# A four-layer graph network on one core: x and the first adjacency matrix are loaded ahead of the later layers' weights, whose preparation moves into the aggregations of three later steps

## The chip, the cores and the metric

The kernel runs on one core of a Trainium2 chip. The metric is the time of one execution on the device in microseconds (us); lower is better. Engines are named as in the profile: PE is TensorE's matmuls and PEld its loads of the stationary operand, DVE is VectorE, ACT ScalarE, POOL GpSimd, SP SyncE (which here only issues DMAs). The prediction below was written from the profile of the kernel before, with the changed kernel not yet built.

## The reference

```python
# x (8, 1024, 128), adj (8, 1024, 1024) of zeros and ones, mask (8, 1024), 4 layers
h = x
for i in range(4):
    hw = einsum('bnc,cd->bnd', h, weight[i])
    m = einsum('bjn,bjd->bnd', adj, hw)
    gx = m @ w_ih[i].T + b_ih[i]
    gh = h @ w_hh[i].T + b_hh[i]
    xr, xz, xn = split(gx, 3)
    hr, hz, hn = split(gh, 3)
    r, z = sigmoid(xr + hr), sigmoid(xz + hz)
    n = tanh(xn + r * hn)
    h = (1 - z) * n + z * h
out = layernorm(x + h * mask[:, :, None])
```

## The kernel before

The kernel forms m @ w_ih.T as (adj.T h) (weight w_ih.T). So a layer needs one joined matrix wx = weight[l] w_ih[l].T and one transposed matrix wh = w_hh[l].T, both 128 x 384, and both are held as a sum of a high part (rounded to the fast fp32r type) and a low part (the rest). The states are split in the same way. An adjacency block is exact in the high part alone; VectorE checks this by OR-ing the bits of every block into `low` (`check_adj`, L720), and a general path at the end runs only if a low bit was set.

Graphs are worked in four pairs, and a pair in 8 steps (`STEPS = 2 * L`): step g works on layer g // 2 of graph g % 2. A step is:

- `aggregate`: S = adj.T h in two banks `p_S`, one for each half of the 1024 nodes, from 8 adjacency blocks of 128 rows. There are 32 products of 512 columns (h high and h low). In steps 0 and 1 of the first pair the blocks are the outer loop (L380, L382), since they are still arriving; elsewhere the halves are (L398).
- ScalarE copies S to `S_hi`, and VectorE forms `S_lo` (`s_low`).
- `transpose_former` (L369): the new state of the step before is transposed back into `p_tr`, for its next aggregation; ScalarE and VectorE split it into `nat_hi` and `nat_lo`.
- `gates`, for each half: 9 products with the state (banks `p_r`, `p_z`, `p_hn`) and 9 with S (L408 to L410). ScalarE takes the sigmoids and the tanh, VectorE forms t (L851, L857), GpSimd forms (h - n) and z (h - n) (L1003, L1007), VectorE adds the new state (`new_state`, L796), and ScalarE and VectorE split it (`h_high`, `h_low`).

Every engine runs its own list of instructions in order, written out by hand, and waits on counted semaphores: `wait_ge(name, n)` holds the engine until n events have been counted. What stands between the main operations are fillers: `fill` on VectorE issues one check of an adjacency block (one after S_lo of half 0, one in the middle of the gates, one at the end of the step), and `take_adj` on ScalarE casts a block from `adj_in` to `adj_hi`. `adj_in` has one buffer for each of the 8 blocks, so block j of the next graph is loaded by SP only when block j of the last one was both cast and checked.

The start, ahead of step 0, in the order of the lists: SP issues the weights of the four layers (`load_layer`, three DMAs each), the rows of biases and the mask, x of graph 0, the 8 adjacency blocks of graph 0, x of graph 1, and then the blocks of graph 1 one by one. TensorE transposes 7 blocks of 128 x 128 for each layer (`transpose_weights`) and multiplies the transposed weight with w_ih (`join_weights`, 384 columns, in full fp32). VectorE copies the transposed matrices to SBUF (`copy_weights`, L689), ScalarE writes the high parts (`split_w_hh`, `split_joined`) and VectorE the low ones. `transpose_x` transposes x (L349), and its parts go to `hT_hi` and `hT_lo` (`take_xT`; `xT_done` counts them). The start uses gate banks and state buffers that are free until then (`p_start`, `places_start`).

In steps 0 and 1 of the first pair ScalarE casts all blocks of graph 0 and the even blocks of graph 1; VectorE casts the odd blocks of graph 1 (`take_adj1`, L731).

Of the kernel before, what the change touches and what calls it, by code (L numbers as in the profile page):

```python
# [32 lines left out]
def gnn_kernel(nc, x, adj, nodemask, weight, w_ih, w_hh, b_ih, b_hh, out):  # L33
# [13 lines left out]
    with ctx:  # L47
# [49 lines left out]
        p_start = [(p_r, p_z), (p_S[0], p_S[1]), (p_hn, p_xn), (p_r, p_z)]  # L97
        p_rows = p_start[L - 1][1][:, G * C:]

        def flat(t):  # L100
# [4 lines left out]
        places_start = [work[:, 0:2].rearrange("p a b c -> p (a b c)")[:, 0:N], hT[:, 1],  # L105
                        y[:, 0].rearrange("p a b -> p (a b)"), y[:, 1].rearrange("p a b -> p (a b)")]
        w_nat = [t[:, 0:(1 + 2 * G) * C].rearrange("p (q d) -> p q d", d=C) for t in places_start]

        w_tr = work[:, 2:4].rearrange("p a b c -> p (a b c)")[:, 0:L * (1 + G) * C].rearrange("p (l d) -> p l d", l=L)
        bias_rows, mask_rows = (t[:, N - P:N] for t in places_start[0:2])  # L110
# [8 lines left out]
        start_joined = sem("start_joined")  # L119
        start_hi = sem("start_hi")  # L120
        start_lo = sem("start_lo")
        rows_out = sem("rows_out")
# [3 lines left out]
        adj1_ready = sem("adj1_ready")  # L126
# [92 lines left out]
        def wait_adj(eng, graph, j, graph1=False):  # L219

            if graph1:
                if j % 2:
                    eng.wait_ge(adj1_ready, j // 2 + 1)
                else:
                    eng.wait_ge(adj_ready, NB + j + 2)
            else:
                eng.wait_ge(adj_ready, NB * graph + j + 1)
# [5 lines left out]
        def _(sp):  # L233
# [5 lines left out]
            for l in range(L):  # L239
                load_layer(l)  # L240
# [24 lines left out]
            def body(p, first, last):  # L265
                if first:

                    sp.wait_ge(start_tr, L)
# [43 lines left out]
        def _(pe):  # L312
            pe.wait_ge(ident_made, 1)

            def transpose_weights(l):
                px, ph = p_start[l]
                pe.wait_ge(w_in[l], 48)
                if l == L - 1:

                    pe.wait_ge(start_lo, 1)  # L320
# [3 lines left out]
                if l == L - 1:  # L324
                    pe.wait_ge(rows_in, 48)
# [86 lines left out]
            def gates(p, g, h, first):  # L412
# [10 lines left out]
                if prior:  # L423
                    pe.wait_ge(r_act, HS * p + k)
# [622 lines left out]
```

## Time and profile before

| | us |
|---|---|
| three runs | 572.51, 572.16, 570.96 |
| median | 572.16 |
| profiled execution, its own time from its first to its last instruction (the span) | 570.9 |
| TensorE busy in it | 544.4 (95%) |
| VectorE busy | 431.5 (76%) |
| ScalarE busy | 302.0 (53%) |
| GpSimd busy | 227.1 (40%) |

The span runs from the first to the last instruction of the only core; no time around it is listed for the profiled execution. It lies at the lower end of the three runs. In a timeline a row gives the start and the duration of an instruction in us; "idle before <-releaser" in brackets is how long its engine stood idle ahead of it and who ended that. Instructions of one engine overlap a little, since the next is begun while the last results of the former are written.

### The profile page before, as it was taken

What the parts mean: (1) busy time and instruction counts of PE and PEld (TensorE: products, weight loads), DVE (VectorE), ACT (ScalarE), POOL (GpSimd) and SP (SyncE); (2) the same over time, 40 slices, a digit from 0 to 9 for tenths busy, and PEclk for the clock granted to TensorE, in tenths of its full rate; (3) what the DMA queues carried; (4) which work ended last, traced back from release to release, by engine and by line L of the source; (5) the groups of instructions that cost most, each with busy time, mean ns of one, the idle gap of its engine ahead of it and who ended that gap; (6) DMA issues with size and microseconds to landing.
All of it is one profiled execution on the core that took longest, in us unless ns stands there. A gap on an engine that the chain in (4) does not pass through costs nothing.

```text
span 570.9 us, 7455 instructions
## 1 busy us (share of the span) xinstructions
PE 544.4 (95%) x2536; PEld 446.3 (78%) x2536; DVE 431.5 (76%) x726; ACT 302.0 (53%) x454; POOL 227.1 (40%) x156
## 2 busy tenths in 40 slices
PE   5899999999999999999999999999999999999970
PEld 4567888888888888888888888888888888888860
DVE  3998787875778888877667889887577898675475
ACT  3864444447775434545876454445877444444432
POOL 0054334443265444433266443333364633433302
PEclk9999999999999999999999999999999999999995
DMA  7972233002500109401600017701520013000002
GB/s 233 394 240 75 74 111 110 1 0 105 191 1 1 39 22 331 127 0 53 243 0 0 0 37 232 245 0 37 174 84 0 2 37 111 0 1 0 1 1 76
DMA packets 38125, 48.39 MB, mean 85 GB/s; under 512 B 1656, under 2 KB 29904, under 8 KB 38096
## 3 DMA queue, kind: packets, MB, share of 16 engines
q1 hardware_dynamic: 38096, 48.02, 25.3%
q8 instruction: 16, 0.26, 0.2%
q14 instruction: 13, 0.11, 0.1%
HBM read 43.82 MB, written 4.19 MB: 84 GB/s over the span
## 4 chain that ended last, share of the span: by engine, by line
PE 89%; DVE 7%; ACT 1%; issue 1%; DMA 1%; SPq 0%; POOL 0%; DVEq 0%; ACTq 0%
PE p_S L398 38%; PE p_r L408 5%; PE p_r L410 5%; PE p_r L409 5%; PE p_z L408 5%; PE p_z L410 5%; PE p_z L409 5%; PE p_tr L369 5%; PE p_hn L408 2%; PE p_hn L410 2%; PE p_hn L409 2%; PE p_xn L408 2%; PE p_xn L410 2%; PE p_xn L409 2%; DVE low L720 2%; PE p_tr L349 1%
## 5 line engine op out<-in xcount | busy, mean ns | idle before, releaser
L1003 POOL TENSOR_TENSOR work<-hT,work 128x512 f32<-128x512 f32 x62 | 99.1, 1598 | 284.1 <-ACT work L565 283.9
L398 PE MATMUL p_S<-adj_hi,nat_hi 128*128 128x512 f32 x480 | 187.4, 390 | 0.0
L398 PE MATMUL p_S<-adj_hi,nat_lo 128*128 128x512 f32 x480 | 186.9, 389 | 0.0
L398 PEld LDWEIGHTS p_S<-adj_hi,nat_hi 128*128 128x128 f32 x480 | 90.1, 188 | 18.6
L398 PEld LDWEIGHTS p_S<-adj_hi,nat_lo 128*128 128x128 f32 x480 | 90.1, 188 | 18.5
L720 DVE TENSOR_TENSOR low<-low,adj_in 128x1024 int32<-128x1024 int32 x64 | 94.3, 1473 | 0.5
L1007 POOL TENSOR_TENSOR work<-work 128x512 f32<-128x512 f32 x62 | 88.4, 1426 | 4.9
L851 DVE SCALAR_TENSOR_TENSOR work<-p_hn,bias,work 128x512 f32<-128x512 f32 x64 | 47.9, 749 | 55.0 <-ACT work L565 55.0
L565 ACT ACTIVATE work<-p_r,bsum 128x512 f32<-128x512 f32 x64 | 44.1, 689 | 73.5 <-PE p_r L410 73.4
L796 DVE TENSOR_TENSOR hT<-work 128x512 f32<-128x512 f32 x64 | 43.9, 686 | 30.4 <-POOL work L1007 30.0
L565 ACT ACTIVATE work<-p_z,bsum 128x512 f32<-128x512 f32 x64 | 44.1, 689 | 41.0 <-PE p_z L410 41.0
L523 ACT ACTIVATE hT_hi<-hT 128x512 fp32r<-128x512 f32 x48 | 30.3, 632 | 65.6 <-DVE hT L796 65.6
L680 DVE TENSOR_TENSOR hT_lo<-hT,hT_hi 128x512 fp32r<-128x512 f32 x48 | 46.8, 975 | 18.8 <-ACT hT_hi L523 16.8
L523 ACT ACTIVATE S_hi<-p_S 128x512 fp32r<-128x512 f32 x64 | 38.0, 593 | 43.2 <-PE p_S L398 38.1
L523 ACT ACTIVATE adj_hi<-adj_in 128x1024 fp32r<-128x1024 f32 x60 | 60.3, 1050 | 0.0
L565 ACT ACTIVATE work<-work,bias 128x512 f32<-128x512 f32 x64 | 46.3, 724 | 22.2 <-DVE work L857 22.2
L680 DVE TENSOR_TENSOR S_lo<-p_S,S_hi 128x512 fp32r<-128x512 f32 x64 | 43.6, 682 | 8.3 <-ACT S_hi L523 8.3
L857 DVE TENSOR_TENSOR work<-p_xn,work 128x512 f32<-128x512 f32 x64 | 43.8, 685 | 5.3
L369 PE MATMUL p_tr<-ident,hT 128*128 128x128 f32 x256 | 38.6, 273 | 3.4 <-DVE hT L796 3.4
L369 PEld LDWEIGHTS p_tr<-ident,hT 128*128 128x128 f32 x256 | 31.7, 140 | 11.7 <-issue 3.6
L995 POOL TENSOR_TENSOR hT<-hT_hi,hT_lo 128x512 f32<-128x512 f32 x16 | 25.7, 1627 | 28.1 <-DVE hT_lo L680 28.1
L680 DVE TENSOR_TENSOR nat_lo<-p_tr,nat_hi 128x512 fp32r<-128x512 f32 x48 | 32.8, 683 | 3.7 <-ACT nat_hi L523 3.4
(130 smaller groups left out, 915.5 us busy)
## 6 DMA issues: line engine op xcount, KB each, us to landing
adj_in<-in_adj_dram SPq DMA_DIRECT2D x64, 512.0 KB, 5.4
x_in<-in_x_dram SPq DMA_DIRECT2D x8, 512.0 KB, 11.2
y<-in_x_dram SPq DMA_DIRECT2D x8, 512.0 KB, 5.0
out_dram<-y SPq DMA_DIRECT2D x7, 512.0 KB, 3.3
out_dram<-y SPq DMA_DIRECT2D x2, 256.0 KB, 3.0
y<-in_L_gnn_w_ih_dram SPq DMA_DIRECT2D x2, 192.0 KB, 3.4
y<-in_L_gnn_w_hh_dram SPq DMA_DIRECT2D x2, 192.0 KB, 4.1
work<-in_L_gnn_w_ih_dram SPq DMA_DIRECT2D x1, 192.0 KB, 2.6
```

Of the source, the lines that this page charges most:

```text
L369: last = nc.tensor.transpose(p_tr[h][:, i, :], hT[:, g % 2, n0:n0 + P], ident[:, :])
L398: last = nc.tensor.matmul(p_S[h][:, :], part[:, s, j], adj_hi[:, s, j, half(h)], start=(j == 0 and part is nat_hi), stop=(j == NB - 1 and ...
L408: nc.tensor.matmul(bank[:, :], w_h[:, l, cols], v_h, start=start, stop=False)
L409: nc.tensor.matmul(bank[:, :], w_h[:, l, cols], v_l, start=False, stop=False)
L410: return nc.tensor.matmul(bank[:, :], w_l[:, l, cols], v_h, start=False, stop=stop)
L523: return nc.scalar.activation(dst, src, ACT.Copy)
L565: nc.scalar.activation(dst, bank, func, bias=b).then_inc(made, 1)
L680: return nc.vector.tensor_tensor(dst, src, hi.bitcast(F32), ALU.subtract)
L720: nc.vector.tensor_tensor(low[:, :], low[:, :], adj_in[:, j].bitcast(I32), ALU.bitwise_or).then_inc(adj_checked, 1)
L851: nc.vector.scalar_tensor_tensor(t_sb[:, h], p_hn[:, :], bias[:, 1, G * l + 2:G * l + 3], r_sb[:, h], ALU.add, ALU.mult).then_inc(t_mul, 1)
L1003: nc.gpsimd.tensor_tensor(t_sb[:, h], hT[:, s, half(h)], n_sb[:, h], ALU.subtract).then_inc(d_sub, 1)
L1007: nc.gpsimd.tensor_tensor(t_sb[:, h], z_sb[:, h], t_sb[:, h], ALU.mult).then_inc(d_mul, 1)
```

## The change

SP loads layer 0's weights, then the adjacency blocks of graph 0, the rows of biases and mask, x of graph 1, layer 1's weights, the blocks of graph 1, and layers 2 and 3 behind them. x of graph 0 is loaded by a DMA that ScalarE issues. Ahead of step 0 only layer 0 is transposed and joined. Layer 1 is done inside the aggregation of step 1, layers 2 and 3 inside those of steps 2 and 3, in the banks `p_tr` and in work or y buffers. The 9 products of step 0's first half with the state stand between the first blocks of the aggregation. The odd blocks of graph 0 are cast by VectorE (`take_odd`), and checks 4 to 7 of graph 0 stand among the work of step 0. The core of the diff:

```diff
-        p_start = [(p_r, p_z), (p_S[0], p_S[1]), (p_hn, p_xn), (p_r, p_z)]
+        p_start = [(p_xn, p_hn)] + [tuple(p[:, :, :].rearrange("p i c -> p (i c)") for p in p_tr)] * (L - 1)
...
# SP
-            for l in range(L):
-                load_layer(l)
+            load_layer(0)
+            for j in range(NB):
+                sp.dma_start(adj_in[:, j], adj_v[0, j]).then_inc(adj_loaded[j], 16)
...
-            sp.dma_start(x_in[:, 0], x_v[0]).then_inc(x_loaded[0], 16)
-            for j in range(NB):
-                sp.dma_start(adj_in[:, j], adj_v[0, j]).then_inc(adj_loaded[j], 16)
-            sp.dma_start(x_in[:, 1], x_v[1]).then_inc(x_loaded[1], 16)
+            sp.dma_start(x_in[:, 1], x_v[1]).then_inc(x_loaded[1], 16)
+            load_layer(1)
             for j in range(NB):
-                wait_adj(sp, 0, j)
+                wait_adj(sp, 0, j, True)
                 sp.wait_ge(adj_checked, j + 1)
                 sp.dma_start(adj_in[:, j], adj_v[1, j]).then_inc(adj_loaded[j], 16)
+            load_layer(2)
+            sp.wait_ge(start_joined, 2)
+            load_layer(3)
...
-                    sp.wait_ge(start_tr, L)
+                    sp.wait_ge(start_joined, L)
...
# TensorE
             transpose_weights(0)
-            transpose_weights(1)
+            transpose_x(0, 0, True)
             join_weights(0)
-            transpose_weights(2)
-            join_weights(1)
-            transpose_weights(3)
-            join_weights(2)
-            transpose_x(0, 0, True)
-            join_weights(3)
...
+                        if s == 0 and j < G:
+                            state_product(p, 0, 0, j, first)
+                        elif s == 1 and j == 3:
+                            pe.wait_ge(xT_done, 4)
+                            transpose_weights(1)
+                        elif s == 1 and j == 6:
+                            join_weights(1)
...
+                        if first and g in (2, 3) and (h, j) == (0, 1):
+                            transpose_weights(g)
                     last.then_inc(s_done, 1)
+                    if first and g in (2, 3) and h == 0:
+                        join_weights(g)
...
+                    if first and h == 0 and g < L:
+                        pe.wait_ge(start_lo, g + 1)
                     transpose_h(p, g - 1, h)
...
# ScalarE
+            act.dma_start(x_in[:, 0], x_v[0]).then_inc(x_loaded[0], 16)
...
-                        places = ((), (0,), (2, 4), (6,)) if first else ((), (4, 5), (6, 7), ())
+                        places = ((), (), (0,), (2,)) if first else ((), (4, 5), (6, 7), ())
...
+                    if first and g == 1:
+                        take_adj(0, 1, 4, True)
+                        split_w_hh(1)
+                        take_adj(0, 1, 6, True)
+                        split_joined(1)
+                    elif first and g in (2, 3):
+                        split_w_hh(g)
                     s_high(p, g, 0)
+                    if first and g in (2, 3):
+                        split_joined(g)
...
+                        if first and k == 0:
+                            split_x(0, 1, True)
...
# VectorE
+                        if first and g == 1:
+                            take_xT(0, 1)
+                            copy_weights(1)
+                            take_odd(1, 7)
+                        elif first and g in (2, 3):
+                            copy_weights(g)
                         new_state(p, g - 1, 1)
                         if first and g == 1:
-                            take_adj1(7)
+                            split_w_hh(1)
+                            split_joined(1)
...
                     s_low(p, g, 0)
+                    if first and g in (2, 3):
+                        split_w_hh(g)
+                        split_joined(g)
+                    if first and g == 0:
+                        take_rows()
...
                     s_low(p, g, 1)
+                    if first and g == 0:
+                        check_adj(0, 0, 4)
...
                             if first and g == 0:
-                                take_adj1(1)
+                                split_x(0, 1)
+                                take_odd(1, 1)
                     if first and g == 0:
-                        take_adj1(3)
+                        check_adj(0, 0, 5)
+                        take_odd(1, 3)
...
                     if first and g == 0:
-                        take_adj1(5)
+                        check_adj(0, 0, 6)
+                        take_odd(1, 5)
+                        check_adj(0, 0, 7)
...
-            for j in range(NB - 2):
-                check_adj(0, 0, j, True)
-            take_xT(0, 0)
+            copy_weights(0)
+            split_x(0, 0)
+            split_w_hh(0)
+            dve.wait_ge(xT_hi, 1)
+            lo(hT_lo[:, 0, half(0)], flat(p_tr[0]), hT_hi[:, 0, half(0)]).then_inc(xT_done, 1)
+            take_odd(0, 1)
+            split_joined(0)
+            dve.wait_ge(xT_hi, 2)
+            lo(hT_lo[:, 0, half(1)], flat(p_tr[1]), hT_hi[:, 0, half(1)]).then_inc(xT_done, 1)
+            take_odd(0, 3)
+            check_adj(0, 0, 0, True)
+            take_odd(0, 5)
+            check_adj(0, 0, 1)
+            take_odd(0, 7)
+            check_adj(0, 0, 2)
+            check_adj(0, 0, 3)
             pairs(dve, body)
...
```

New or changed helpers that it calls:

```python
def take_rows():                       # VectorE
    dve.wait_ge(rows_tr, 1)
    nc.vector.tensor_copy(bias[:, :, :].rearrange("p a b -> p (a b)"), p_rows[:, 0:2 * L * G])
    nc.vector.tensor_copy(mask[:, :], p_rows[:, 2 * L * G:2 * L * G + B * NB]).then_inc(rows_out, 1)
    dve.wait_ge(rows_out, 1)
    nc.vector.tensor_tensor(bsum[:, :], bias[:, 0], bias[:, 1], ALU.add).then_inc(rows_out, 1)

def split_w_hh(l):                     # VectorE
    dve.wait_ge(start_hh, l + 1)
    lo(wh_lo[:, l], p_start[l][1][:, 0:G * C], wh_hi[:, l])

def split_joined(l):                   # VectorE
    dve.wait_ge(start_hi, l + 1)
    lo(wx_lo[:, l], p_start[l][0][:, 0:G * C], wx_hi[:, l]).then_inc(start_lo, 1)

def take_odd(graph, j):                # VectorE
    dve.wait_ge(adj_loaded[j], 16 * (graph + 1))
    nc.vector.tensor_copy(adj_hi[:, graph, j], adj_in[:, j]).then_inc(adj_odd, 1)
```

## Rows read from the trace of the kernel before

**Rows 1.** The page of the kernel before, part 1: busy time and share by engine.

```profile
PE 544.4 (95%) x2536; PEld 446.3 (78%) x2536; DVE 431.5 (76%) x726; ACT 302.0 (53%) x454; POOL 227.1 (40%) x156
```

**Rows 2.** Windows, 55.5 to 540 us. Stretch, length, busy by engine, PEclk, DMA share, GB/s.

```profile
55.50:72.00 16.50, 16.50 (x79) 13.60 (x78) 13.29 (x16) 7.57 (x13) 6.60 (x5) 1.00 0.29 96
120.00:540.00 420.00, 420.00 (x1969) 347.39 (x1969) 317.49 (x539) 232.43 (x345) 181.78 (x122) 1.00 0.21 70
```

**Rows 3.** Timeline of the start, all engines. Start, duration (us), engine, line, operation, idle.

```profile
4.78 0.88 PE L322 MATMUL p_r<-ident,work 128*128 128x128 f32 x3 [4.78 <-DMA work<-in_L_gnn_w_hh_dram]
...
6.62 0.69 DVE L689 COPY work<-p_r 128x512 f32<-128x512 f32 x1 [4.65 <-PE p_z L331]
...
9.68 0.85 PE L322 MATMUL p_hn<-ident,y 128*128 128x128 f32 x3
...
14.50 0.81 PE L337 MATMUL p_hn<-work 128*128 128x384 f32 x2
...
17.42 4.86 ACT L523 ACTIVATE adj_hi<-adj_in 128x1024 fp32r<-128x1024 f32 x5
...
18.60 7.87 DVE L720 TENSOR_TENSOR low<-low,adj_in 128x1024 int32<-128x1024 int32 x6
```

**Rows 4.** Timeline of TensorE (PE), 25 to 75 us.

```profile
25.99 0.39 PE L382 MATMUL p_S<-adj_hi,nat_lo 128*128 128x512 f32 x1
...
29.37 0.39 PE L408 MATMUL p_r<-S_hi,wx_hi 128*128 128x512 f32 x1
...
43.32 0.50 PE L380 MATMUL p_S<-adj_hi,nat_hi 128*128 128x512 f32 x1 [1.77 <-DVE adj_hi L731]
...
46.18 0.60 PE L369 MATMUL p_tr<-ident,hT 128*128 128x128 f32 x4
...
55.34 0.39 PE L398 MATMUL p_S<-adj_hi,nat_hi 128*128 128x512 f32 x1
...
62.60 0.60 PE L369 MATMUL p_tr<-ident,hT 128*128 128x128 f32 x4
...
71.75 0.39 PE L398 MATMUL p_S<-adj_hi,nat_hi 128*128 128x512 f32 x1
```

**Rows 5.** Timeline of VectorE (DVE), 27 to 92 us.

```profile
34.86 1.79 DVE L731 CAST adj_hi<-adj_in 128x1024 fp32r<-128x1024 f32 x1
...
40.59 1.00 DVE L680 TENSOR_TENSOR hT_lo<-hT,hT_hi 128x512 fp32r<-128x512 f32 x1 [0.70 <-ACT hT_hi L523]
...
59.18 2.31 DVE L720 TENSOR_TENSOR low<-low,adj_in 128x1024 int32<-128x1024 int32 x1
...
61.41 0.68 DVE L796 TENSOR_TENSOR hT<-work 128x512 f32<-128x512 f32 x1
62.02 0.68 DVE L680 TENSOR_TENSOR S_lo<-p_S,S_hi 128x512 fp32r<-128x512 f32 x1
...
63.40 1.22 DVE L720 TENSOR_TENSOR low<-low,adj_in 128x1024 int32<-128x1024 int32 x1
...
66.80 0.75 DVE L851 SCALAR_TENSOR_TENSOR work<-p_hn,bias,work 128x512 f32<-128x512 f32 x1 [0.98 <-ACT work L565]
...
77.76 0.68 DVE L796 TENSOR_TENSOR hT<-work 128x512 f32<-128x512 f32 x1
```

**Rows 6.** Windows of the start, the same columns as Rows 2.

```profile
0.00:4.00 4.00, 0.00 (x0) 0.00 (x0) 0.97 (x2) 1.49 (x2) 0.75 (x7) 1.00 0.42 123
3.00:4.00 1.00, 0.00 (x0) 0.00 (x0) 0.00 (x0) 0.00 (x0) 0.00 (x0) 1.00 0.96 284
16.00:22.00 6.00, 5.45 (x23) 3.44 (x22) 5.79 (x9) 6.00 (x8) 0.00 (x0) 1.00 1.03 419
```

**Rows 7.** Timeline of ScalarE (ACT), the first S_hi.

```profile
26.02 0.60 ACT L523 ACTIVATE S_hi<-p_S 128x512 fp32r<-128x512 f32 x1 [0.88 <-PE p_S L382]
```

**Rows 8.** DMA issues between 48 and 70 us: transfer, count, KB each, us to landing.

```profile
adj_in<-in_adj_dram SPq DMA_DIRECT2D x4, 512.0 KB, 3.2
```

**Rows 9.** Timeline of GpSimd (POOL), the operation ahead of 61.41.

```profile
58.79 1.62 POOL L1007 TENSOR_TENSOR work<-work 128x512 f32<-128x512 f32 x1
```

More of the change, by code:

```diff
@@ L410, in product, with state_product, gates @@
                 return nc.tensor.matmul(bank[:, :], w_l[:, l, cols], v_h, start=False, stop=stop)
-            def gates(p, g, h, first):
+            def state_product(p, g, h, q, first):
                 l, s = divmod(g, 2)
                 k = 2 * g + h
-                if l == 0:
-                    pe.wait_ge(xT_done, 4 * p + k + 1)
-                else:
-                    pe.wait_ge(h_split, HS_IN * p + k - 4 + 1)
-                state = (hT_hi[:, s, half(h)], hT_lo[:, s, half(h)])
+                if q == 0:
+                    if l == 0:
+                        pe.wait_ge(xT_done, 4 * p + k + 1)
+                    else:
+                        pe.wait_ge(h_split, HS_IN * p + k - 4 + 1)
+                    if first and k == 0:
+                        pe.wait_ge(start_lo, 1)
+                if not (first and k == 0):
+                    pe.wait_ge((r_act, z_act, t_mul)[q], HS * p + k)
+                state = (hT_hi[:, s, half(h)], hT_lo[:, s, half(h)])
+                last = product((p_r, p_z, p_hn)[q], (wh_hi, wh_lo), l, q, state, True, q == G - 1)
+                if q == G - 1:
+                    last.then_inc(hn_done, 1)
+            def gates(p, g, h, first, begun=False):
+                l, s = divmod(g, 2)
+                k = 2 * g + h
                 fed = (S_hi[:, h], S_lo[:, h])
                 prior = not (first and k == 0)
-                if prior:
-                    pe.wait_ge(r_act, HS * p + k)
-                product(p_r, (wh_hi, wh_lo), l, 0, state, True, False)
-                if prior:
-                    pe.wait_ge(z_act, HS * p + k)
-                product(p_z, (wh_hi, wh_lo), l, 1, state, True, False)
-                if prior:
-                    pe.wait_ge(t_mul, HS * p + k)
-                product(p_hn, (wh_hi, wh_lo), l, 2, state, True, True).then_inc(hn_done, 1)
+                if not begun:
+                    for q in range(G):
+                        state_product(p, g, h, q, first)
                 pe.wait_ge(s_split, HS * p + k + 1)
@@ L459, in body @@
                     if g == 0 and first:
-                        pe.wait_ge(start_lo, L)
-                        pe.wait_ge(rows_out, 2)
+                        transpose_rows()
                     for h in range(2):
                         transpose_former(p, g, h, first)
-                        gates(p, g, h, first)
+                        gates(p, g, h, first, first and g == 0 and h == 0)
             pairs(pe, body)
@@ L530, in split_w_hh @@
                 act.wait_ge(start_tr, l + 1)
[L531 to L534 removed]
+                copy(wh_hi[:, l], p_start[l][1][:, 0:G * C]).then_inc(start_hh, 1)
             def split_joined(l):
@@ L542, in take_adj @@
                 act.wait_ge(adj_loaded[j], 16 * (2 * p + s + 1))
-                copy(adj_hi[:, s, j], adj_in[:, j]).then_inc(adj_ready, 2 if first and s == 1 else 1)
+                copy(adj_hi[:, s, j], adj_in[:, j]).then_inc(adj_ready, 2 if first else 1)
             def split_x(p, s, first):
@@ L618, in body @@
                             take_former(p, g - 1, 1)
+                        if first and k == 0:
+                            split_x(0, 1, True)
                         gate(n_sb[:, h], t_sb[:, h], t_add, n_act, ACT.Tanh, bias[:, 0, G * l + 2:G * l + 3], p, k)
@@ L812, in body @@
                 checks = [(p, 1, j) for j in range(NB)] + [(p + 1, 0, j) for j in range(NB) if not last]
-                if first:
-                    checks = [(0, 0, NB - 2), (0, 0, NB - 1)] + checks
                 def fill(g):
-                    if checks and (g or (first and checks[0][1] == 0)):
+                    if checks and g:
                         check_adj(*checks.pop(0))
@@ L840, in body @@
                     s_low(p, g, 1)
+                    if first and g == 0:
+                        check_adj(0, 0, 4)
                     for h in range(2):
```

95 lines of the change are left out of this document (37 added, 58 removed).

## The prediction

> **What bounds the kernel now.** I read the page first: TensorE is busy 95% of the span, VectorE 76% [rows 1]. That is a mean, so I cut the span into stretches. From 55.5 us on TensorE has no gap at all: 16.50 of 16.50 us, and 420.00 of 420.00 later [rows 2]. So a microsecond that TensorE loses or wins ahead of the gate products of step 3 (numbered from 0) reaches the end whole, and nothing behind it gives it back. Up to 55.5 us it idles: first it waits for the weights (4.78 us), then the first aggregation ends late, and the second stops 1.77 us for a cast on VectorE [rows 3, 4]. In the timeline of VectorE the reader is to see the checks of adjacency blocks: six in a row take 7.87 us, a lone one takes 1.22, and one that meets a GpSimd operation 2.31 us [rows 3, 5].
>
> **The sum is made on TensorE's marks** [rows 4]: gate products of step 1 begin (with a transposition) at 46.18, step 2's aggregation at 55.34 (9.16 later), its gates at 62.60 (7.26 later), step 3's aggregation at 71.75.
>
> **Part 1, start to the first aggregation.** Layer 0's weights (0.46 MB) now share the DMA engines with x (0.52 MB), issued by ScalarE. Such an issue isn't in the trace. Bounds: the weights land at 4.78 as before, or after all 0.98 MB; some 0.49 MB (123 GB/s over 4 us) had moved by 4.0 us and 0.28 MB go per us then [rows 6], so 5.7. I take 5.6, since both move rows of 128 floats, and 6.5 for x. The Trainium skill ("DMA: Bandwidth & Descriptors", Issuing engines are not separate DMA queues) says that transfers of several issuing engines interleave on the same DMA engines; by it 5.6 is nearer than 4.78, and no row of this trace shows two issuers.
>
> TensorE: 7 weight and 8 x transpositions at the slow rate, 0.21 us each (0.85 for 3 with the latency of the last, 0.42) [rows 3], the join between; done by 9.6. ScalarE: nat_hi 1.0, wh_hi 0.5, two halves of x transposed (waiting for TensorE) to 9.5, then the cast of block 0, 0.97 (4.86 for five), so the aggregation begins near 10.5. It has 32 products and now 9 state products between them: 41 at 0.2275 (7.26 us for 32 [rows 4]) is 9.3 us, and 1.0 more for what still runs at the slow clock: end 20.8. The blocks don't bound it: 5.17 MB in all, the last 4.2 at 0.42 MB per us (419 GB/s) [rows 6], land by about 16.1. VectorE's list ahead of it is copy 0.7, nat_lo 1.15, three splits of weights and two of x (2.7), four casts (2.4), four checks (4.9), with one GpSimd wait, from 7.4 to some 19.7: no bound either. Before, the last of these products started at 25.99 [rows 4]. So far the gain is some 5.6 us, and because the 9 state products are done, the first product on S starts near 21.8 where it started at 29.37: 7.6 us earlier.
>
> **Part 2, to the end of step 1's aggregation: VectorE takes most of it back.** Only 4 of 8 checks are done by then, and the casts and splits come in between. Behind block 3 of step 1 TensorE now waits for xT_done 4 ahead of the transpositions of layer 1's weights. On VectorE that split stands behind everything of step 0. It starts at 21.15 (half 0 ends some 0.3 before half 1, and S_hi takes 0.60 [rows 7]). A 512-wide operation is followed after 0.61 by the next (61.41, 62.02 [rows 5]), so: two S_lo 1.2, the bias rows 0.4 (three small ones), two pairs of t operations 2.9 (0.75 and 0.68, with small gaps [rows 5]), nat_lo 1.2, checks 4 to 7 at 1.15 4.6, casts 1, 3, 5 at 0.6 1.8, state 0.6, its split 0.65, two splits of x transposed 1.2: 14.6 us. Waits: a cast took 1.79 and a check 2.31 where GpSimd runs, 1.1 to 1.2 more than alone [rows 5]; two of the seven such operations give 2.1 us, since GpSimd has four operations in this stretch. For ScalarE it waits 1.0 (nat_hi of x 1 and the state's split, the latter as 0.70 before [rows 5]). Sum 17.7: xT_done 4 at 38.8. Bounds: 35.7 with no wait, 43 if each of the seven pays 1.1.
>
> Behind it TensorE does 7 transpositions (4 took 0.60 with the latency of the last [rows 4]; I take 0.9 with the change of mode), blocks 4 to 7 (3.64) and the join (0.32; a pair had 0.81 with latency [rows 3]): end 43.6. Block 7's load follows check 7 (37.6) by 3.2 [rows 8], its cast ends at 41.7, no bound. The joined product goes through ScalarE (0.5) and VectorE (0.5), on which the next transposition waits (start_lo 2): 43.95 against 46.18 before. **Gain 2.2 us.** The unfilled rest is a new idle stretch of TensorE: block 2's cast on ScalarE stands behind the new state's split and ends near 35.0, while block 1 is done at 30.8.
>
> **Part 3, steps 2 and 3: TensorE pays in the solid stretch.** Each aggregation gets 7 transpositions behind block 1 and the join behind half 0. The join waits for copy_weights(g), which stands on VectorE behind the check that closes the former step. In the trace that check starts at 59.18, is held by GpSimd's operation of 58.79 to 60.41, and what follows starts at 61.41, 6.07 us after the aggregation began at 55.34; in the next step 77.76, 6.01 after 71.75 [rows 4, 5, 9]. These marks hang on TensorE's own last gates, so they move with it. The copy takes 0.69 [rows 3] and the join can start at 6.85; TensorE is there at 3.64 + 0.75 = 4.4. Stall 2.4 us, nothing is left behind it to fill it. Aggregation then: 6.85 + 0.35 + 3.64 = 10.8 against 7.26: **3.6 us for each step, 7.2 for both.** Of this 2.3 is the moved work itself. Bounds: no stall 2.3; nothing in the rows lets it be over 2 x 3.6 while VectorE's order stands. The splits (start_lo) are ready at 9.0, ahead of 10.8, so the gates don't wait.
>
> **What costs nothing.** Layer 2's loads follow check 7 and land before step 2 (3 to 6 us of cover); layer 3's wait for the second join, near 43, and land by 48, 20 us ahead of use. The loads of y and of graph 2 now stand on SP's queue behind the fourth join (about 80 us) instead of the fourth transposition; the first reader of graph 2 is the check that ends step 3, at about 96, and a load takes some 3 to 6 us. The x loads behind them wait for graph 1's last check, as before. If that cover were gone, a VectorE wait of a few us would come in step 3.
>
> **Sum:** -2.2 + 7.2 = +5.0 on the profiled execution's span of 570.9, so 575.9. Its span lies 1.3 below the median of the runs shown, 572.16; the forecast for a median is 577.1.
>
> **Rivals.**
> 1. *The clock falls* (14%). At the start a transposition had 0.42 us of latency and 0.21 of pace, later 4 of them have 0.60 in all [rows 3, 4]: the low and the high level, 1.2 and 2.4 GHz, though the granted clock reads 1.00 in both [rows 2, 6]. The 1.77 us gap at 43.3 didn't bring the low level back [rows 4]. The new gap of about 4 us (30.8 to 35.0) and the one of 2 us after it are longer. If the low level comes back, the 4.9 us of work from 38.8 to 43.6 takes up to twice as long, and with the other gaps I price it at 3 to 5: 581. The Trainium skill ("TensorE: Matmul & The Clock Gate", Why this matters for your kernels) warns that a long idle gap between bursts throttles the clock again. By that rule this rival is the forecast; no row here has a gap so long.
> 2. *The joins are not late* (13%): VectorE reaches each copy within 3.6 us of the aggregation's start, because the closing check meets no GpSimd operation and its predecessor no wait. For: the 1.1 us of lock is removable. Against: that alone gives 5.0, still 0.6 too late. Then +2.3 - 2.2 = +0.1: 572.3, no change.
> 3. *Other side: VectorE doesn't hold step 1* (9%). With xT_done 4 ready by 32 us, the start-up gain of 7.6 would reach step 2 but for the moved layer 1 work. It decides from there: 6.8 us earlier than 38.8 turns +5.0 into -1.8. Then 570 or a little less. Against: 14.6 us of bare work start at 21.15, so this needs both a much earlier aggregation and work that I count twice.
> 4. *More locks* (12%): every check and cast of step 1 meets GpSimd: xT_done 4 up to 43, gain 2.2 turns into a loss of 2: 581.
>
> **Chances.** Forecast, 575 to 580: 52%. Rival 1 14, rival 4 12, rival 2 13, rival 3 9. About 0.3%, 1.7 us, is what a measurement of this kernel tells from no change. Faster: rival 3 and a little of 2, 10%. Same: the rest of 2 and the low edge, 14%. Slower 76%. The range 572.0 to 581.5 leaves out rival 3 and the far ends of 1 and 4.
>
> **What would show it.** Right: first aggregation product near 10.5 us; a TensorE gap of 3 to 4 us before block 2 of step 1 for ScalarE's adj_hi, and another for hT_lo ahead of the weights' transpositions near 38 us; gates of step 1 near 44; then in each of steps 2 and 3 one gap of about 2.4 us ahead of the 384-column join, released by VectorE's copy, and aggregations 10.8 long; no gap later. Wrong: those two gaps missing (the copy came early), TensorE at half rate behind 35 us, or gates of step 1 at 40 or earlier.

## The result and the profile after

| | us |
|---|---|
| kernel before, five runs beside it | 572.16 median (570.86 to 572.85) |
| changed kernel, five runs | 580.25 median (579.88 to 583.26) |
| ratio | 1.0159, 95% interval 1.014 to 1.0178 |
| span of the profiled execution (583.26, the slowest of the five) | 581.4 |

Slower by 8.1 us: inside the range of 572.0 to 581.5, 3.1 above the forecast, and just above the band of 575 to 580 that the forecast's chance was given for. A run's time is its span and 1.8 us around it. So the profiled execution before, with a span of 570.9, was one of about 572.7 us, 0.6 above the median of 572.16, and not at the lower end of the runs, as it had seemed; the forecast is not moved by this, since its sum is a difference. The page of the changed kernel, busy time and the row of the granted clock over 40 slices:

```profile
PE 547.6 (94%) x2536; PEld 449.7 (77%) x2536; DVE 434.1 (75%) x730; ACT 298.4 (51%) x450; POOL 226.8 (39%) x156
...
PEclk9979899999999999999999999999999999999995
```

TensorE is busy 3.2 us longer than in [rows 1] for the same 2536 instructions, so 7.3 of the 10.5 us between the two spans are time in which it stands idle. Slices 3 and 5 of the clock's row (29 to 44 and 58 to 73 us) show where it also ran slowly. Windows of those stretches and of the rest (columns as in [rows 2]):

```profile
36.00:44.00 8.00, 6.86 (x21) 5.30 (x22) 5.52 (x8) 4.22 (x7) 2.50 (x2) 0.57 0.58 177
44.00:60.00 16.00, 15.71 (x77) 12.68 (x76) 11.87 (x17) 8.42 (x15) 4.57 (x3) 1.00 0.12 35
60.00:68.00 8.00, 5.80 (x18) 4.03 (x17) 7.34 (x9) 1.60 (x3) 1.61 (x1) 0.79 0.01 2
...
100.00:540.00 440.00, 440.00 (x2063) 364.35 (x2063) 338.16 (x562) 241.59 (x360) 188.91 (x125) 1.00 0.22 71
```

From 100 us on TensorE is solid, as before. Timeline of TensorE:

```profile
6.59 0.87 PE L324 MATMUL p_xn<-ident,work 128*128 128x128 f32 x3 [6.59 <-DMA work<-in_L_gnn_w_hh_dram]
...
11.74 0.70 PE L375 MATMUL p_S<-adj_hi,nat_hi 128*128 128x512 f32 x1 [0.44 <-ACT adj_hi L538]
...
22.49 0.51 PE L415 MATMUL p_r<-S_hi,wx_hi 128*128 128x512 f32 x1 [0.59 <-DVE S_lo L698]
...
37.06 0.79 PE L375 MATMUL p_S<-adj_hi,nat_hi 128*128 128x512 f32 x1 [5.05 <-ACT adj_hi L538]
...
40.92 0.90 PE L324 MATMUL p_tr<-ident,y 128*128 128x128 f32 x3
...
45.44 0.81 PE L333 MATMUL p_tr<-y 128*128 128x384 f32 x2
...
47.47 0.63 PE L364 MATMUL p_tr<-ident,hT 128*128 128x128 f32 x4 [0.29 <-issue]
...
63.38 1.64 PE L333 MATMUL p_tr<-y 128*128 128x384 f32 x2 [2.20 <-DVE y L707]
...
65.25 0.63 PE L401 MATMUL p_S<-adj_hi,nat_lo 128*128 128x512 f32 x1
65.68 0.63 PE L401 MATMUL p_S<-adj_hi,nat_hi 128*128 128x512 f32 x1
...
69.45 0.60 PE L364 MATMUL p_tr<-ident,hT 128*128 128x128 f32 x4
...
85.33 0.91 PE L333 MATMUL p_tr<-y 128*128 128x384 f32 x2 [2.14 <-DVE y L707]
...
89.76 0.60 PE L364 MATMUL p_tr<-ident,hT 128*128 128x128 f32 x4
```

These are the marks of [rows 4]: the first product on S came at 22.49 (before 29.37), the gates of step 1 at 47.47 (46.18), of step 2 at 69.45 (62.60), of step 3 at 89.76 (79.00). Behind that mark 491.6 us are left, before 491.9: nothing is given back. Three of the four gaps foretold are there: 5.05 us for ScalarE's `adj_hi` in step 1 (3 to 4 had been forecast), and 2.20 and 2.14 ahead of the joins of steps 2 and 3, for VectorE's copy. The fourth, for `hT_lo` near 38 us, is not: behind the first gap blocks 2 and 3 run at half rate and last until the transpositions at 40.92. The products at 65.25 and 65.68 stand 0.43 apart instead of 0.23, and the granted clock of 60 to 68 us is 0.79: TensorE at its low level, 1.2 GHz, behind a gap. VectorE's timeline in steps 0 to 2:

```profile
27.69 1.79 DVE L745 CAST adj_hi<-adj_in 128x1024 fp32r<-128x1024 f32 x1
...
31.98 1.75 DVE L745 CAST adj_hi<-adj_in 128x1024 fp32r<-128x1024 f32 x1
33.66 1.74 DVE L810 TENSOR_TENSOR hT<-work 128x512 f32<-128x512 f32 x1
...
39.58 1.28 DVE L698 TENSOR_TENSOR hT_lo<-p_tr,hT_hi 128x512 fp32r<-128x512 f32 x2
...
60.43 2.30 DVE L734 TENSOR_TENSOR low<-low,adj_in 128x1024 int32<-128x1024 int32 x1
62.65 0.68 DVE L707 COPY y<-p_tr 128x512 f32<-128x512 f32 x1
```

The last two are the stall: the copy of layer 2's weights behind a closing check of 2.30 us. The first three, two casts and the new state, are prolonged from 0.7 us each while GpSimd works. The timeline of GpSimd has the operation that the closing check met, and that of ScalarE the arrival of x, and the cast that ends the long gap:

```profile
60.04 1.61 POOL L1050 TENSOR_TENSOR work<-work 128x512 f32<-128x512 f32 x1
```

```profile
5.29 1.06 ACT L538 ACTIVATE nat_hi<-x_in 128x1024 fp32r<-128x1024 f32 x1 [2.54 <-DMA x_in<-in_x_dram]
...
35.44 0.63 ACT L538 ACTIVATE hT_hi<-hT 128x512 fp32r<-128x512 f32 x1 [3.74 <-DVE hT L810]
35.97 1.04 ACT L538 ACTIVATE adj_hi<-adj_in 128x1024 fp32r<-128x1024 f32 x1
```

A check alone takes 1.22 [rows 5]. The Trainium skill ("SBUF — State Buffer", Who interferes with whom) says that a VectorE operation with two SBUF inputs contends with a GpSimd operation that reads SBUF. The trace agrees: GpSimd ends at 61.65, and the check, which began at 60.43, ends 1.08 later.

### The profile page after: what moved, and what is told of

Its sections match the earlier page's. It is cut to its first block, busy times and chain, and to the rows that moved or that the text cites. A ratio compares the mean times of both kernels' runs of the same rounds, so it can differ in the third digit from the quotient of the medians.

```text
span 581.4 us, 7459 instructions
## 1 busy us (share of the span) xinstructions
PE 547.6 (94%) x2536; PEld 449.7 (77%) x2536; DVE 434.1 (75%) x730; ACT 298.4 (51%) x450; POOL 226.8 (39%) x156
## 4 chain that ended last, share of the span: by engine, by line
PE 88%; DVE 6%; ACT 2%; issue 1%; DMA 1%; POOL 1%; SPq 0%; DVEq 0%; POOLq 0%
PE p_S L401 36%; PE p_r L415 5%; PE p_r L417 5%; PE p_r L416 5%; PE p_z L415 5%; PE p_z L417 5%; PE p_z L416 5%; PE p_tr L364 5%; PE p_hn L415 2%; PE p_hn L417 2%; PE p_hn L416 2%; PE p_xn L416 2%; PE p_xn L415 2%; PE p_xn L417 2%; DVE low L734 1%
## 5 line engine op out<-in xcount | busy, mean ns | idle before, releaser
L401 PE MATMUL p_S<-adj_hi,nat_hi 128*128 128x512 f32 x480 | 189.4, 395 | 0.0
L538 ACT ACTIVATE adj_hi<-adj_in 128x1024 fp32r<-128x1024 f32 x56 | 56.7, 1049 | 2.1 <-DMA adj_in<-in_adj_dram 2.1
```

Source lines behind the costliest of these rows:

```text
L401: last = nc.tensor.matmul(p_S[h][:, :], part[:, s, j], adj_hi[:, s, j, half(h)], start=(j == 0 and part is nat_hi), stop=(j == NB - 1 and ...
L538: return nc.scalar.activation(dst, src, ACT.Copy)
```

## The experiments

All marks in one table: start of the gates of steps 1, 2 and 3 in the profiled execution, its span, and the median of the runs. Behind the gates of step 3 every kernel here has 490.7 to 491.9 us left, so an edit is worth what the third mark shows.

| kernel | step 1 | step 2 | step 3 | span | median |
|---|---|---|---|---|---|
| before | 46.18 | 62.60 | 79.00 | 570.9 | 572.16 |
| changed | 47.47 | 69.45 | 89.76 | 581.4 | 580.25 |
| changed, a second execution profiled | 46.92 | 67.33 | 87.61 | 579.2 | |
| copies early | 46.59 | 64.75 | 82.80 | 574.4 | 575.85 |
| block 2 first | 48.02 | 70.05 | 90.36 | 581.4 | 583.15 |
| step 1 reordered | 46.06 | 68.00 | 88.28 | 579.8 | 580.95 |
| gaps filled | 47.17 | 67.53 | 87.80 | 578.5 | 580.11 |
| copies early, step 1 reordered | 45.81 | 63.97 | 82.03 | 573.5 | 575.45 |
| short checks | 43.43 | 63.81 | 84.08 | 575.5 | 578.29 |
| casts on ScalarE | 43.85 | 61.96 | 80.02 | 571.8 | 573.60 |
| checks ahead of x | 47.06 | 65.17 | 83.26 | 574.9 | 576.50 |
| layer 2 in step 1 | 43.53 | 59.95 | 78.02 | 569.4 | 571.13 |

### Copies ahead of the closing check

```diff
 # VectorE: step g, behind its last gate work
+                    if first and g in (1, 2):
+                        copy_weights(g + 1)
                     fill(g)                      # the closing check
...
-                        elif first and g in (2, 3):
-                            copy_weights(g)
```

> Edit: VectorE's copies of the transposed weights of layers 2 and 3 stand ahead of the check that closes the step before, not behind it. Theory 1 (the joins wait for that order): the two stalls ahead of the 384-column join (2.20 and 2.14 us in the profile after) go, and with the first of them the half-rate stretch behind it (about 1.9 us): 574 to 576 us, from 580.25. Theory 2 (the join would wait anyway, for the copy itself or for GpSimd, and only the moved work costs): less than 1 us. Theory 3 (the gap goes but the clock falls all the same, since it hangs on something else in step 2): 576 us with a half-rate stretch left in step 2.

Median 575.85 (575.12 to 576.23), ratio to before 1.0069 (1.005 to 1.0087): 4.4 us off the changed kernel. VectorE and TensorE in step 2, two timelines:

```profile
59.60 0.68 DVE L707 COPY y<-p_tr 128x512 f32<-128x512 f32 x1
60.20 1.70 DVE L734 TENSOR_TENSOR low<-low,adj_in 128x1024 int32<-128x1024 int32 x1
```

```profile
60.33 0.91 PE L333 MATMUL p_tr<-y 128*128 128x384 f32 x2
60.79 0.69 PE L401 MATMUL p_S<-adj_hi,nat_hi 128*128 128x512 f32 x1
61.32 0.39 PE L401 MATMUL p_S<-adj_hi,nat_lo 128*128 128x512 f32 x1
```

The join has no gap ahead of it, and step 2's aggregation lasts 9.0 us (55.75 to 64.75). So the stall is two times 2.2 us, and what is left over the 7.26 of before [rows 4], 1.7 for each layer, is the moved work itself: transpositions 0.68, and 0.09 until the products have their pace again; 0.15 ahead of the join; 0.46 of join; and 0.53 instead of 0.23 from the product behind it to the next.

### Block 2 cast first, and step 1 reordered

Two edits of step 1 alone. The first moves ScalarE's cast of block 2 ahead of the gate work that waits for VectorE; the second does that too, puts VectorE's two last checks and the split of x ahead of the new state, copies layer 1's weights at once, and lets ScalarE take x and block 6 ahead of the state's high part.

```diff
 # ScalarE, both
-                        places = ((), (), (0,), (2,)) if first else ...
+                        places = ((), (), (0, 2), ()) if first else ...
 # VectorE, the second
+                        check_adj(0, 0, 6)
+                        check_adj(0, 0, 7)
+                        take_xT(0, 1)
+                        take_odd(1, 5)
+                        copy_weights(1)
                     new_state(p, g, 0)
...
```

> Edit: ScalarE casts block 2 of graph 1 right behind block 0, in the middle of step 0's gates. The gap of 5.05 us ahead of block 2 then ends some 7 us earlier. Theory 1 (VectorE's split of x transposed, xT_done 4, ends last in step 1): the gap moves behind block 3 and the time stays within 0.7 us of 580.25. Rival (ScalarE's order is what makes step 1 late): the gates of step 1 begin 3 to 5 us earlier, 575 to 577 us.

> Edit: as the one with block 2 early, and besides on VectorE checks 6 and 7 and the split of x transposed stand right behind the cast of block 3, with layer 1's copy, ahead of the new state and its split; ScalarE takes x transposed and block 6 ahead of the state's high part. Theory 1 (the order of VectorE's list sets step 1): xT_done 4 near 37 instead of 40.9, gates of step 1 near 42 to 43 instead of 47.5, and no or a short half-rate stretch: 575 to 576.5 us. Rival (VectorE's amount of work sets it, not the order): gates of step 1 at 46 to 47, 579 to 580.

Block 2 first: median 583.15 (582.33 to 585.69), ratio 1.0205 (1.0178 to 1.0232). TensorE's timeline, and a window from it:

```profile
41.08 0.90 PE L324 MATMUL p_tr<-ident,y 128*128 128x128 f32 x3 [5.96 <-DVE hT_lo L698]
```

```profile
38.00:42.00 4.00, 0.92 (x5) 0.92 (x6) 3.03 (x5) 0.15 (x1) 1.49 (x2) 0.50 0.62 181
```

The gap only moved behind block 3, and its releaser is now the split of x: VectorE, not ScalarE's order, holds step 1. It was 2.9 us worse than the changed kernel, where 0.7 at most had been expected: the half rate (0.50 to 42, 0.76 in the four us behind) now falls on the transpositions and block 4, behind which no wait is left to absorb it (4.91 us from transposition to join instead of 4.52 and 3.59 in the two profiles of the changed kernel), and in step 2 it came too.

Step 1 reordered: median 580.95 (579.62 to 581.64), ratio 1.0155 (1.0132 to 1.0178), no gain; gates of step 1 at 46.06, earlier than in the changed kernel but not 42 to 43, and in step 2 the half rate came again (21.94 us). VectorE's timeline:

```profile
33.94 3.64 DVE L736 TENSOR_TENSOR low<-low,adj_in 128x1024 int32<-128x1024 int32 x2
37.50 1.28 DVE L700 TENSOR_TENSOR hT_lo<-p_tr,hT_hi 128x512 fp32r<-128x512 f32 x2
```

Two checks, 2.4 alone, met GpSimd and took 3.64, so x was split only 2.1 us earlier; behind a gap of 3.57 the transpositions and block 4 ran at half rate.

### Idle gaps filled with useless products

```diff
 # TensorE: 20 products behind block 1 of step 1, 8 behind block 3, 9 ahead of each later join
+            def idle_products(g, n):
+                pe.wait_ge(r_act, 2 * g)
+                for _ in range(n):
+                    nc.tensor.matmul(p_r[:, :], nat_hi[:, g % 2, 0], adj_hi[:, g % 2, 0, half(0)],
+                                     start=True, stop=True)
```

> Edit: every wait stays; TensorE runs useless products where it idled: 20 behind block 1 of step 1, 8 behind block 3, 9 ahead of the join in each of steps 2 and 3 (they go to a bank that the next gates begin anew, so the output is unchanged). Theory (the gaps let the clock fall, and that costs by itself): no half-rate stretch behind 20 us, and 576.5 to 578 us, some 1.5 from step 1 and 1.9 from step 2. Rival (the half rate falls into time that is waited anyway): the stretch is gone and the time stays at 580, or is over it where a gap was shorter than its filling.

Median 580.11 (579.73 to 580.4), ratio 1.0144 (1.0124 to 1.0165). Windows of step 1 and step 2:

```profile
31.00:38.00 7.00, 6.43 (x29) 5.01 (x28) 6.30 (x6) 3.11 (x5) 3.00 (x2) 1.00 0.22 75
60.00:68.00 8.00, 7.83 (x36) 6.00 (x36) 6.95 (x9) 1.88 (x4) 1.39 (x1) 1.00 0.00 0
```

The granted clock is 1.00 in both stretches and the half rate is gone. The span is 2.9 under the first profile of the changed kernel, but the medians differ by 0.1: the clock cost up to 3 us in that one execution and next to nothing in the typical one. The useless products are not quite free of effect (the gates of step 1 come at 47.17, in the second profile of the changed kernel at 46.92), so a gain of some tenths could hide behind them. My expectation of 576.5 to 578 fell.

### Both repairs, and the checks cut short

The first of these joins the edits "copies early" and "step 1 reordered". The second takes the work of four checks away:

```diff
-                nc.vector.tensor_tensor(low[:, :], low[:, :], adj_in[:, j].bitcast(I32),
+                w = 8 if (isinstance(p, int) and p == 0 and s == 0 and j >= HB) else N
+                nc.vector.tensor_tensor(low[:, 0:w], low[:, 0:w], adj_in[:, j, 0:w].bitcast(I32),
```

> Edit: the copies of layers 2 and 3 ahead of the closing checks, and the reordered step 1, together. The step-1 order alone began step 1's gates at 46.06 us but kept both stalls; the early copies alone gave 575.85. Theory 1 (the two are separate stretches and add up): gates of step 1 near 45 to 46, steps 2 and 3 at 18.1 us each, 574.5 to 576 us. Rival (the reordered lists cost something later that hid behind the stalls): 577 or over.

> Edit, on the changed kernel: checks 4 to 7 of graph 0 look at 8 columns of their block instead of 1024, so that part of the bit check is left out (the output on this input doesn't depend on it); every wait and every other instruction stays. Theory 1 (the amount of VectorE work that stands ahead of xT_done 4, and of block 7's load, sets step 1): VectorE has about 4 us less there, xT_done 4 at 36 to 37.5 instead of 40.9, gates of step 1 at 42.5 to 44, and 575 to 577 us from 580.25. Rival (the loads or ScalarE set step 1): gates of step 1 over 46, 579 to 580.5.

> The changed kernel itself, for a second profile. Its profiled execution was 3 us above its other four (583.26 against 579.88 to 580.59). Theory (the half-rate stretches cost time only in some executions, by where they end): here a time near 580.2, with a half-rate stretch in step 1 whose loss lies ahead of the wait for xT_done 4, and little or none behind the first join. Rival (the profile's 3 us are something else): the same half-rate stretches and another place with the difference.

Both repairs: 575.45 (574.91 to 576.41), ratio 1.0072 (1.0058 to 1.0087), the same as the copies alone within their spread.

Short checks: 578.29 (577.28 to 580.63), ratio 1.0135 (1.0115 to 1.0155). TensorE's timeline, then VectorE's:

```profile
36.76 0.55 PE L324 MATMUL p_tr<-ident,y 128*128 128x128 f32 x3 [1.02 <-DVE hT_lo L698]
```

```profile
33.57 1.25 DVE L735 TENSOR_TENSOR low<-low,adj_in 128x8 int32<-128x8 int32 x1
...
41.10 0.69 DVE L746 CAST adj_hi<-adj_in 128x1024 fp32r<-128x1024 f32 x1 [2.63 <-DMA adj_in<-in_adj_dram]
```

Three of the checks took 0.15 or 0.16 us; the fourth, though it looks at 8 columns only, took 1.25, since it met GpSimd. Against the second profile of the changed kernel x was split 4.4 us earlier (36.71 instead of 41.08) and the gates of step 1 came 3.5 earlier, at 43.43. Then the load of block 7 ended last. The median fell by 2.0 only, where 3 to 5 had been expected: the profiled execution was the fastest of five. The two longest (579.66 and 580.63) have a mean granted clock of 0.983 against its 0.989, but one of 578.12 has 0.984, so that alone does not explain it.

The second profile of the unaltered changed kernel, TensorE's timeline:

```profile
41.13 0.55 PE L324 MATMUL p_tr<-ident,y 128*128 128x128 f32 x3
...
62.91 0.91 PE L333 MATMUL p_tr<-y 128*128 128x384 f32 x2 [2.22 <-DVE y L707]
...
67.33 0.60 PE L364 MATMUL p_tr<-ident,hT 128*128 128x128 f32 x4
```

This run took 581.0. Behind the same gap of 2.2 us the clock stayed at 1.00: step 2 took 20.41 instead of 21.98, and that is where most of the 2.2 us between the two spans lies (0.55 of it in step 1). VectorE's cast of block 7 stood 1.75 us for its load there and started at 44.59, and the new state and the splits of layer 1 stand behind it.

### Casts on ScalarE, and the checks ahead of x

On top of the early copies, ScalarE casts blocks 2, 3, 5 and 7 of step 1 and copies layer 1's weights, VectorE splits x right behind check 5, and the join stands behind block 5. In the second kernel checks 6 and 7 come ahead of the split of x again, so that their blocks are loaded sooner.

```diff
 # ScalarE, step 1
+                        take_xT(0, 1)
+                        take_odd(3)
                         take_adj(0, 1, 4, True)
...
+                        copy(w_tr[1], p_start[1][0][:, 0:(1 + G) * C]).then_inc(start_copied, 1)
                         split_w_hh(1)
+                        take_odd(5)
+                        h_high(0, 0, 0)
+                        split_joined(1)
                         take_adj(0, 1, 6, True)
+                        take_odd(7)
...
 # VectorE, step 0; the second kernel has take_xT(0, 1) last of these four
                         check_adj(0, 0, 5)
-                        take_odd(1, 3)
+                        take_xT(0, 1)
+                        check_adj(0, 0, 6)
+                        check_adj(0, 0, 7)
```

> Edit, on the kernel with early copies: ScalarE, idle for 9 us there, casts blocks 2, 3, 5 and 7 of graph 1 and copies layer 1's transposed weights; VectorE does checks 5, 6, 7 and x transposed right behind step 0's t operations; the join of layer 1 stands behind block 5. Theory 1 (VectorE's list sets step 1): xT_done 4 near 35, gates of step 1 at 43 to 44.5, 572.5 to 574.5 us, about the kernel before (571.8): the moved work of 1.7 us in each of steps 2 and 3 eats what step 1 wins. Rival (the load of block 7, which waits for check 7, sets it whatever VectorE drops): gates of step 1 at 45 or later, 575 to 576.

> Edit, on the kernel with ScalarE's casts (573.6): VectorE does checks 6 and 7 ahead of the split of x transposed, so that GpSimd's additions for x, which start at that split, don't meet the checks (two checks took 4.47 us there), and block 7's load starts earlier. Theory (block 7's load behind check 7 sets the end of step 1): check 7 ends 1 to 1.7 us earlier, gates of step 1 at 42.2 to 43.2 instead of 43.85, 572 to 573.2 us. Rival (xT_done 4, now later, sets it): gates of step 1 at 44 or later, no gain.

Casts on ScalarE: 573.6 (573.28 to 574.87), ratio 1.0044 (1.0029 to 1.0059). Three timelines, VectorE, GpSimd and TensorE:

```profile
33.47 4.47 DVE L746 TENSOR_TENSOR low<-low,adj_in 128x1024 int32<-128x1024 int32 x2
```

```profile
34.59 4.50 POOL L1046 TENSOR_TENSOR hT<-hT_hi,hT_lo 128x512 f32<-128x512 f32 x2
```

```profile
34.75 0.49 PE L324 MATMUL p_tr<-ident,y 128*128 128x128 f32 x3
...
41.67 0.50 PE L375 MATMUL p_S<-adj_hi,nat_hi 128*128 128x512 f32 x1 [2.14 <-ACT adj_hi L538]
```

Splitting x early frees GpSimd to start on it, and it then runs against the two checks: 4.47 us for 2.4. The new state behind them took 1.77 and ended at 39.6, ScalarE's split of it waits 2.03 us for that, and behind it in ScalarE's list stands the cast of block 6, for which TensorE waits 2.14. x is there in time, and VectorE holds step 1 by another way.

Checks ahead of x: 576.5 (576.48 to 576.73), ratio 1.0081 (1.0067 to 1.0095), 2.9 worse, where I had expected a gain. TensorE's timeline, then ScalarE's:

```profile
37.95 0.90 PE L324 MATMUL p_tr<-ident,y 128*128 128x128 f32 x3 [2.91 <-DVE hT_lo L710]
```

```profile
39.74 0.60 ACT L538 ACTIVATE y<-p_tr 128x512 f32<-128x512 f32 x1 [5.00 <-PE p_tr L327]
...
43.98 2.00 ACT L538 ACTIVATE adj_hi<-adj_in 128x1024 fp32r<-128x1024 f32 x2
```

Three checks in a row took 5.66 (31.03 to 36.7), the transpositions waited 2.91 and ran at half rate, and ScalarE stood 5.00 us at its copy with the casts of blocks 5, 6 and 7 queued behind it.

### Layer 2 prepared in step 1's idle time

If the moved work costs only where TensorE is solid, then in step 1's gap it is free. On top of the last kernel, layer 2 is loaded right behind layer 1, and transposed and joined in the banks `p_xn` and `p_hn` ahead of the wait for x; only layer 3 stays in step 3. ScalarE's casts of blocks 6 and 7 stand ahead of `split_joined(1)`.

```diff
 # TensorE, step 1 behind block 3
+                            pe.wait_ge(t_mul, 2)
+                            pe.wait_ge(t_add, 2)
+                            transpose_weights(2)
+                            join_weights(2)
                             pe.wait_ge(xT_done, 4)
                             transpose_weights(1)
```

> Edit, on that one: layer 2's weights are loaded behind layer 1's and transposed and joined in step 1's idle time of TensorE, in the gate banks that are free there; ScalarE copies them; step 2 has no such work. Theory (moved work costs where TensorE is solid, 1.7 us in a step, and nothing where it idles): step 2 back at 16.4 us, gates of step 1 within 0.5 us of the former, 570.3 to 571.8 us, level with or just below the kernel before (571.3). Rival (the lists of VectorE and ScalarE in step 1 are too full for it): gates of step 1 over a microsecond later, 572 or more.

Median 571.13 (570.75 to 571.91, 11 runs) against 572.16 (570.58 to 572.83, 15 runs): ratio 0.9988 (0.9979 to 0.9998). That is level with the kernel before, or just below it: its own median lay between 571.34 and 572.16 in the batches of runs beside the experiments. TensorE's timeline and a window:

```profile
36.57 0.91 PE L334 MATMUL p_xn<-y 128*128 128x384 f32 x2 [0.69 <-ACT y L543]
...
38.03 0.55 PE L325 MATMUL p_tr<-ident,y 128*128 128x128 f32 x3 [0.56 <-DVE hT_lo L719]
...
43.53 0.61 PE L365 MATMUL p_tr<-ident,hT 128*128 128x128 f32 x4
...
59.95 0.60 PE L365 MATMUL p_tr<-ident,hT 128*128 128x128 f32 x4
```

```profile
38.00:42.00 4.00, 3.96 (x20) 3.27 (x21) 3.75 (x6) 3.17 (x6) 2.44 (x2) 1.00 0.31 123
```

x is split no sooner than in the last kernel (37.98 and 37.90), but the wait is filled with layer 2, the clock stays at 1.00, and ScalarE's casts are no longer stuck. Of the 3.5 us by which the gates of step 1 come earlier than in the last kernel, 2.1 lie between the transpositions of layer 1 and the join, where that one had the half rate and a wait for block 5, and 1.5 behind the join, where it waited for block 6. Filling the gap and the new order of ScalarE's casts came in one edit, so their shares are not separated. Step 2 takes 16.42 again, exactly as before [rows 4]; step 3, which still carries layer 3, 18.07. Against the kernel before that is -2.65 at the gates of step 1, nothing in step 2, +1.67 in step 3: -1.0, the difference of the medians.

## Why the prediction was right, and where its sizes were off

The marks that carry the sum came as forecast in kind: a gain at the start, most of it lost again while VectorE holds step 1, and a stall ahead of each join. The typical execution (the second profile) has a span of 579.2 and misses the sum of 575.9 by 3.3 us: 2.97 at the gates of step 1, 0.67 in steps 2 and 3, less 0.31 behind them. These misses add up, so the number is not right by misses that cancel. But one of my signs of being wrong did appear, the half rate behind 35 us, and 580.25 lies so near the 581 of rivals 1 and 4 that the median alone does not tell them from the forecast; the marks and the experiments do.

**Part 1** was right to 0.7 us. The weights landed at 6.59, not 5.6, and so outside my bounds of 4.78 and 5.7. ScalarE's x, which I had let land last, at 6.5, was there first, at 5.3. My upper bound counted the two loads alone, 0.98 MB; but at 9, 290 and 313 GB/s in three windows of 2 us the core had moved 1.22 MB by 6.0. The rest is most likely the adjacency blocks, which SP issues from 2.20 on, and their share the reason for the delay; no run tests it. The delay passed on: first product of the aggregation 11.74 (10.5), first product on S 22.49 (21.8). The gain to there was 6.9 us of the 7.6.

**Part 2** named the right holder but was the term most mis-sized: the gates of step 1 came at 47.47 instead of 43.95, a loss of 1.3 where the sum had a gain of 2.2. The 3.5 us in the first profile: x was split at 40.86, not 38.8 (0.6 from the later start, 1.1 because three operations were prolonged by GpSimd and not two, the third being the new state, which was not among my seven; 0.4 scattered); 0.9 because transpositions and the first products behind them ran at half rate (4.52 us from transposition to join, 3.59 in the second profile; 3.6 in my sum); and 0.5 because join to gates took 2.03, not 1.5. In the second profile the last is 2.2, the clock costs nothing behind 41.1, and the sum of the misses is 3.0. Block 7's load, no bound in my sum with a cast ended at 41.7, was later than that too: its cast ended at 44.64 and 45.28 in the two profiles, and in the second one VectorE's last split of layer 1, which the gates wait for, began 0.2 us later for it.

That VectorE held step 1 is shown by the short checks: less work on it alone moved the mark by 3.5. ScalarE's cast of block 2, where the long gap was, was not the cause (block 2 first). But VectorE was not the only one: a DMA (short checks), block 6's cast (casts on ScalarE) and ScalarE's queue (checks ahead of x) stood close behind it. That fits with how little the shifts of single operations gained in step 1.

**Part 3** was right in its mechanism. The stall was 2.20 and 2.14 (2.4 in the sum), and removing both gave 4.4 on the medians. The moved work was mis-sized: 1.7 us for each step, not 1.15. I had taken the join at 0.35 from a pair of start-up joins; in the solid stretch it costs 0.15 + 0.46 + 0.30 = 0.91. Together 3.9 for each step, 7.8 where the sum had 7.2.

**The clock (rival 1)** came on top and did not take the forecast's place. It fell behind the long gap of step 1, but in the changed kernel its half rate then mostly covers blocks 2 and 3, and without it TensorE would only have waited longer at the transpositions. It cost 0.9 in step 1 and 1.6 in step 2 in the first profile; with the gaps filled, the median stayed as it was. The Trainium skill ("TensorE: Matmul & The Clock Gate", Why this matters for your kernels) warns of a long idle gap between bursts. The trace agrees at 5.05 us; the gap of 2.2 us went one way in one execution and the other way in another.

**Rivals 2 to 4.** The joins were late, against rival 2. Rival 3 fell, since x was split at 40.86 and not by 32. Rival 4 was there in part: x was split about half way between my 38.8 and its 43, but only 1.1 us of that is one prolonged operation more. The loads of layers 2 and 3, of y and of graph 2 cost nothing, as said.

The typical execution, by the second profile: +0.7 at the gates of step 1, +4.0 and +3.9 in steps 2 and 3, 8.6 in all, and 0.3 less behind them. The medians say 8.1; this run, 581.0, lies 0.75 above its median, and the one profiled before about 0.6 above its own. What stays open is which executions lose their clock behind a gap of 2.2 us, and what the short checks' missing 1.5 us are: the traces of its two longest runs were not taken.

## What to carry to other kernels

Work moved out of a start-up that other engines bound is free only where it meets idle time of the same engine; in a solid stretch each piece costs its full length and the change of mode on both sides, and one late operand in front of it adds a stall that nothing refills. Before such a move, ask in which gap the piece would fit, and put the copy that its second half waits for ahead of work that nobody waits for yet, here the closing check. When one engine's list holds a stage, look at the second and third to end before reordering it: here single shifts gave between -4.4 and +2.9 us. The way back to the time before took all of it together: 4.4 us from the early copies, 2.3 from ScalarE's casts, and 2.5 from the use of the gap.

## What the runs showed of the hardware

- Behind idle gaps of 5.05, 5.96, 3.57 and 2.91 us TensorE's products stood 0.43 us apart instead of 0.23, the granted clock 0.50 to 0.62 from 38 to 42 us; behind the gap of 2.20 to 2.22 us in step 2 it happened in three traces (1.6 us lost in each) and not in two others (the second profile and the short checks), and never behind one of 2.13 to 2.15. With useless products in the gaps the clock stayed at 1.00.
- A fall of the clock cost nothing where its stretch ended in a wait anyway: the second profile of the changed kernel has 0.68 from 36 to 44 us, the one with filled gaps 1.00. VectorE's split of x starts at 39.80 and 39.76 in them, and the transpositions that wait for it at 41.13 and 41.10.
- Two checks that met GpSimd took 3.64 or 4.47 us instead of 2.4, depending on what GpSimd had to do just then; an earlier result for GpSimd can so delay VectorE. The prolonging does not shrink with the operation: a check of 8 columns took 1.25 us instead of 0.15.
- Loads issued by two engines at the start did not land in proportion: the 0.52 MB issued by ScalarE at 0.74 were there at 5.3, the 0.46 MB issued by SP from 0.74 to 2.2 at 6.6. Before, with only SP issuing and the next layers' weights behind them, they had landed at 4.78 [rows 3].
